# First stages of a three-block decoder kernel: the scan placed ahead of the last matrix powers, token weights computed in two halves, and the compression rows of batch 0 stored and loaded back ahead of the others

## Chip, cores and metric

The kernel runs on one core of a Trainium2 chip. The metric is device time in microseconds (us) of one execution, as the median of several. Times of single instructions come from a profile of one execution.

## What is computed

Three blocks follow each other, each ending in a layer normalisation over 256 features: an attention over 8192 key rows chosen by top-8, a cross attention with 16 heads, and a feed-forward block with token-to-expert selection. The change touches only the opening of the first block, which is (16 batches, 256 tokens, 256 features):

```python
xB = jnp.einsum('bsd,de->sbe', x, Bm)
def step(h, u):
    h = h @ A + u
    return (h, None)
h_final, _ = jax.lax.scan(step, h0, xB)
h_proj = h_final @ W_imp.T
importance = jax.nn.softmax(jnp.einsum('bsd,bd->bs', x, h_proj), axis=-1)
token_pref = jax.nn.softmax(jnp.einsum('bsd,nd->bsn', x, W_router), axis=-1)
neuron_w = jnp.einsum('bs,bsn->bn', importance, token_pref)
neuron_w = neuron_w / (neuron_w.sum(-1, keepdims=True) + 1e-08)
shared_compress = jnp.einsum('bn,ndr->bdr', neuron_w, compress)
Q = jnp.einsum('bsd,bdr->bsr', x, shared_compress)
scores = jnp.einsum('bsr,nr->bsn', Q, K) / math.sqrt(K.shape[1])
topk_scores, topk_idx = jax.lax.top_k(scores, kk)
```

## The kernel before

Every engine has its own instruction list, written out by hand, and waits on semaphores. The names: PE is TensorE, DVE VectorE, ACT ScalarE, POOL GpSimd, SP SyncE, which here only issues DMAs.

**The scan without a loop over 256 steps.** With RAD = 16, the scan is two sums of 16 terms. PE computes powers of A by doubling (`power(r)`, r = 0 to 7; r 0 to 3 give A to A^16, r 4 to 7 powers of A^16), and DVE copies each out of the accumulator before the next can start. `bm_powers` multiplies Bm by the first powers (`Bm_A_pow`), ACT copies. The first sum ("scan1", 32 matmuls over the input `xT_by_step`) gives `scan_partial`; the second ("scan2", 16 small ones with `A16_pow`) gives the final state. `warm(n)` issues n matmuls of 128x128 whose result nobody reads.

**Importance and router.** From the final state PE makes h_proj, then the importance logits ("imp", 32 matmuls). DVE takes their maximum, ACT the exponential, DVE the reciprocal and the product; PE transposes the result. Beside it runs the router: `router(n)` for four quarters n (two groups of batches by two token halves t), ACT copies it out (`router_out`), PE transposes it back, DVE takes the maximum and subtracts it, ACT takes the exponential (`router_exp`), DVE sums it (`router_sum`). Quarters 0 and 1 belong to token half t = 0, quarters 2 and 3 to t = 1. DVE multiplies importance by the reciprocal of the sum into `token_weight_diag`, for both halves, and PE sums over tokens ("nw", 32 matmuls, 16 for each half). A short chain on DVE and PE normalises that into `neuron_diag`.

**Compression.** 32 matmuls over eight loads of `compress` give, for each of 16 batches, two rows of 128x128 values: partition 32c + q of the result holds row q = 2 batch + k, for c = 0 to 3 (quarters of the row). ACT and DVE copy it in eight steps into `scs`, which lies in the space of `xT_by_step`. SP stores it to the DRAM tensor `shared_compress` (`scd`) with eight DMAs of 32 partitions (two halves by four c), and then loads the two rows of one batch back as `sc_in` in the shape in which PE needs it (`scd_v[0]` for batch 0, later one for each batch). Behind that load SP issues the loads of the projection weights.

**The main loop.** Turns c = -4 to 16 work on batches c, c+1, c+2 at once. The first thing that turn -2 does is `shared_q(0)`, which needs `sc_in` and `xT_in`; then come the 32 score blocks of batch 0 (three matmuls of 512 columns each), which ACT copies into `score_row` and of which DVE takes eight best per 2048 keys (`cand_val`, `cand_idx`). In the same turn ACT casts the six weight chunks (`weight_hi`), in order between its score copies: blocks 0 to 3, chunks 0 and 1, blocks 4 to 7, chunks 2 and 3. Three score banks lie between PE and ACT.

## Time and profile before

| | us |
|---|---|
| median of 3 runs | 1390.09 |
| lowest and highest | 1389.33 and 1392.59 |
| profiled execution | 1391.58 |
| span of its instructions | 1389.8 |
| PE busy | 1327.0 (95% of the span) |
| DVE busy | 1122.6 (81%) |
| ACT busy | 719.0 (52%) |
| POOL busy | 727.0 (52%) |

The page gives busy time per engine. "PEclk" or "granted clock" is the share of full speed that TensorE's clock gate passed; full is 2.4 GHz, half 1.2 GHz. The chain of waits follows the last instruction back to what released it, so it shows at each time which engine set the pace. An fp32 matmul stands in the trace as two passes, so 32 matmuls are "x64". The idle time behind "<-" is what the engine waited before an instruction and who ended that wait.

### The profile page before, as it was taken

What the parts mean: (1) busy time and instruction counts of PE and PEld (TensorE: products, weight loads), DVE (VectorE), ACT (ScalarE), POOL (GpSimd) and SP (SyncE); (2) the same over time, 40 slices, a digit from 0 to 9 for tenths busy, and PEclk for the clock granted to TensorE, in tenths of its full rate; (3) what the DMA queues carried; (4) which work ended last, traced back from release to release, by engine and by line L of the source; (5) the groups of instructions that cost most, each with busy time, mean ns of one, the idle gap of its engine ahead of it and who ended that gap; (6) DMA issues with size and microseconds to landing.
All of it is one profiled execution on the core that took longest, in us unless ns stands there. A gap on an engine that the chain in (4) does not pass through costs nothing.

```text
span 1389.8 us, 25203 instructions
## 1 busy us (share of the span) xinstructions
PE 1327.0 (95%) x9839; PEld 995.5 (72%) x9839; DVE 1122.6 (81%) x1627; ACT 719.0 (52%) x1377; POOL 727.0 (52%) x1009
## 2 busy tenths in 40 slices
PE   9856999999999999999999999999999999999898
PEld 4444868686868686868687868777878676867775
DVE  1459889898989898998898889898989986546567
ACT  1443565555555555555555555555555544336564
POOL 0543374747474746464646565656565646342434
PEclk9988999999999999999999999999999999999999
DMA  9462112222222222222223222212221216002412
GB/s 373 145 202 61 57 54 58 71 57 71 61 68 62 69 60 76 60 70 57 65 54 86 57 65 59 73 56 68 59 73 45 73 42 179 1 17 93 154 39 85
DMA packets 57548, 110.36 MB, mean 79 GB/s; under 512 B 9438, under 2 KB 38102, under 8 KB 56278
## 3 DMA queue, kind: packets, MB, share of 16 engines
q1 hardware_dynamic: 40342, 62.17, 14.7%
q0 software_dynamic: 14848, 41.96, 10.8%
q10 hardware_dynamic: 2240, 4.63, 0.9%
q8 instruction: 78, 1.28, 0.4%
q14 instruction: 40, 0.33, 0.1%
HBM read 98.50 MB, written 10.22 MB: 78 GB/s over the span
## 4 chain that ended last, share of the span: by engine, by line
PE 74%; DVE 13%; another core or an unknown queue 4%; POOL 3%; issue 3%; ACT 2%; DMA 1%; SPq 0%; POOLq 0%; ACTq 0%; DVEq 0%
PE side_bank L379 43%; PE score_bank L379 27%; DVE cand_val L1146 4%; DVE cand_idx L1149 4%; DVE x_sum L1172 2%; PE score_bank L748 2%; POOL exp L1397 1%; POOL v_rows L1369 1%; PE side_bank L748 1%; DVE den_recip L1197 1%; DVE top_weight L1168 1%; DVE dispatchedT L1307 1%; ACT exp L904 1%; DMA kT<-den_scratch 0%
## 5 line engine op out<-in xcount | busy, mean ns | idle before, releaser
L892 ACT COPY score_row<-score_bank 128x512 f32<-128x512 f32 x512 | 299.0, 591 | 112.9 <-PE score_bank L379 58.2
L1369 POOL DMA_INDIRECT v_rows<-in_V,top_idx x256 | 249.1, 973 | 130.3 <-issue 74.7
L1146 DVE MAX8 cand_val<-score_row 128x8 f32<-128x2048 f32 x128 | 291.7, 2279 | 30.1 <-ACT score_row L892 27.8
L1149 DVE FIND_INDEX8 cand_idx<-cand_val,score_row 128x8 uint32<-128x2048 f32 x128 | 292.5, 2285 | 0.0
L1397 POOL TENSOR_SCALAR exp<-exp,exp_bound 128x256 f32<-128x256 f32 x512 | 246.9, 498 | 85.6 <-ACT exp L904 84.0
L379 PE MATMUL score_bank<-keysT_hi,qT_hi 128*128 128x512 f32 x512 | 217.2, 424 | 20.6 <-ACT score_row L892 19.1
L379 PE MATMUL score_bank<-keysT_lo,qT_hi 128*128 128x512 f32 x512 | 205.2, 401 | 0.0
L379 PE MATMUL score_bank<-keysT_hi,qT_lo 128*128 128x512 f32 x512 | 204.7, 400 | 0.0
L904 ACT ACTIVATE exp<-side_bank 128x512 f32<-128x512 f32 x256 | 139.1, 595 | 94.4 <-PE side_bank L379 84.5
L379 PE MATMUL side_bank<-qT_heads,kT 64*128 64x256 f32 x1024 | 146.1, 404 | 3.4 <-ACT exp L904 3.4
L1172 DVE SCALAR_TENSOR_TENSOR x_sum<-v_rows,top_weight,x_sum 128x256 f32<-128x256 f32 x256 | 137.0, 535 | 9.4 <-DMA v_rows<-in_V,top_idx 0.3
L379 PEld LDWEIGHTS score_bank<-keysT_hi,qT_hi 128*128 128x128 f32 x512 | 97.8, 191 | 62.0 <-ACT score_row L892 24.3
L909 ACT COPY qT_heads<-side_bank 128x512 f32<-128x512 f32 x128 | 75.1, 587 | 111.5 <-PE side_bank L379 96.1
L379 PE MATMUL side_bank<-exp,v 128*64 128x256 f32 x1024 | 126.7, 388 | 1.1 <-POOL exp L1397 0.8
L379 PEld LDWEIGHTS side_bank<-qT_heads,kT 64*128 64x128 f32 x1024 | 88.6, 187 | 52.4 <-issue 40.9
L379 PE MATMUL side_bank<-wo,qT_heads 128*128 128x256 f32 x512 | 115.7, 379 | 0.8 <-ACT kT L909 0.8
L379 PEld LDWEIGHTS score_bank<-keysT_hi,qT_lo 128*128 128x128 f32 x512 | 98.0, 191 | 23.8
L1418 POOL TENSOR_TENSOR qT_heads<-qT_heads,kT 128x1024 f32<-128x1024 f32 x31 | 74.5, 2404 | 71.0 <-DMA kT<-den_scratch 70.2
L379 PEld LDWEIGHTS score_bank<-keysT_lo,qT_hi 128*128 128x128 f32 x512 | 98.2, 192 | 15.7
L379 PEld LDWEIGHTS side_bank<-wo,qT_heads 128*128 128x128 f32 x512 | 96.9, 190 | 15.3 <-issue 1.4
L1197 DVE RECIPROCAL den_recip<-score_bank 128x256 f32<-128x256 f32 x32 | 56.0, 1749 | 61.6 <-remote 52.8
L379 PEld LDWEIGHTS side_bank<-exp,v 128*64 128x64 f32 x1024 | 67.5, 137 | 52.4 <-issue 21.8
(200 smaller groups left out, 2282.1 us busy)
## 6 DMA issues: line engine op xcount, KB each, us to landing
kT<-den_scratch SPq DMA_DIRECT2D x62, 256.0 KB
...
keysT_raw<-in_KmT ACTq DMA_DIRECT2D x8, 512.0 KB, 10.6
...
```

The lines of the kernel that those rows point to most:

```text
L379: return nc.tensor.matmul(o, l, r, start=start, stop=stop, skip_group_check=True)
L748: last = nc.tensor.transpose(set2[n % 3][:, c0:c0 + P], dtt[:, n, k, :, g], idn[:, :])
L892: nc.scalar.copy(srow[n // PER % 2][:, i * CB:(i + 1) * CB], scb[n % 3]).then_inc(sem("score_evac"), 1)
L904: nc.scalar.activation(ex[i % NEX][:, :, :].rearrange("p k s -> p (k s)"), sp_[o][:, :], ACT.Exp, scale=A_SCALE).then_inc(sem("exp_done"), 1)
L909: nc.scalar.copy(to, job_bank(key)[:, :]).then_inc(free(key), 1)
L1146: own(nc.vector.max(cv[:, tile, cs], srow[g % 2][:, :]))
L1149: nc.vector.max_index(ci[:, tile, cs], cv[:, tile, cs], srow[g % 2][:, :]).then_inc(sem("cand_done"), 1)
L1172: own(nc.vector.scalar_tensor_tensor(acc[:, tile, :], vg[:, k, :], w8[:, tile, k:k + 1], acc[:, tile, :], ALU.mult, ALU.add))
L1197: nc.vector.reciprocal(rden[:, :], den).then_inc(sem("rden_done"), 1)
L1369: pool.indirect_dma_start(out=vg[:, k, :], out_offset=None, in_=V_rows, in_offset=bass.IndirectOffsetOnAxis(ap=i8[:, tile, k:k + 1], axis=0))\
L1397: last = nc.gpsimd.tensor_scalar(ex[i % NEX][:, k, :], ex[i % NEX][:, k, :], ub[:, k, c:c + 1], E_LO, ALU.min, ALU.max)
L1418: nc.gpsimd.tensor_tensor(qt[:, hs, :], qt[:, hs, :], kt[:, hs, :], ALU.mult)\
```

## The change

It changes the order of the lists and how the compression rows are stored; the arithmetic is the same.

- PE: both `bm_powers` come before `power(4)`, the scan is split in two (steps 0 to 7, 8 to 15) with `power(6)` between, and `power(7)` and `router(1)` come after it. `router(3)` moves behind h_proj, the transpose of quarter 2 into the middle of the importance matmuls. Of the early `warm` matmuls three are taken out; new ones stand before the importance transposes (3), before the transpose of neuron weights (3) and behind the compression (16).
- DVE: `scan_partial` is copied before the copy of `power(7)`. Reciprocal and token weights are computed by halves; the half t = 0 stands before `router(3)`.
- ACT: the key loads are issued before `router_out(1)`.
- SP: `xT_in` is loaded before `compress`. Each store is split into rows of batch 0 (2 partitions) and the other 30 partitions; `sc_in` waits for the 8 small stores, and the second half's large stores are issued behind it. The wait for all stores moves to SP before the turns and to ACT at turn -1, away from DVE. `kT` and `qT_heads` are allocated first among the main loop's tiles, which puts them over the space from which the stores read.
- The wait for all eight parts of `keysT_lo` becomes one wait per part at the first score blocks.

```diff
@@ -309,21 +309,29 @@
             for q in range(4):
                 h, bs = q // 2, slice(q % 2 * 8, q % 2 * 8 + 8)
                 sp.dma_start(xs[:, :, h, bs, :], xTs[:, :, h, bs, :]).then_inc(sem(f"xs_in{q}"), 16)
+            sp.dma_start(xt[:, :, :], xT[:, :, 0:S]).then_inc(sem("xt_in"), 16)
             for g in range(NG_SC):
                 sp.dma_start(comp_at[g], comp[:, g * CH:(g + 1) * CH]).then_inc(sem(f"comp_in{g}"), 16)
+            def store_rows(half, r0, r1, done):
+
+                for c in range(4):
+                    sp.dma_start(scd_st[half, c][r0:r1], scs[32 * c + r0:32 * c + r1, half * CH:(half + 1) * CH])\
+                        .then_inc(sem(done), 16)
+
             for half in range(2):
                 sp.wait_ge(sem("sc_act"), 2 * half + 2)
                 sp.wait_ge(sem("sc_dve"), 2 * half + 2)
-                for c in range(4):
-                    sp.dma_start(scd_st[half, c], scs[32 * c:32 * c + 32, half * CH:(half + 1) * CH])\
-                        .then_inc(sem("sc_stored"), 16)
-            sp.dma_start(xt[:, :, :], xT[:, :, 0:S]).then_inc(sem("xt_in"), 16)
-            sp.wait_ge(sem("sc_stored"), 16 * NG_SC)
+                store_rows(half, 0, KT, "sc0_stored")
+                if half == 0:
+                    store_rows(0, KT, B * KT, "sc_stored")
+            sp.wait_ge(sem("sc0_stored"), 16 * 8)
             sp.dma_start(sct[:, :, :], scd_v[0]).then_inc(sem("sct_in"), 16)
+            store_rows(1, KT, B * KT, "sc_stored")
             for n, (w, i, k) in enumerate(WCHUNKS):
                 sp.dma_start(wraw[:, 1, i, k, :], w[:, k * INNER:(k + 1) * INNER]).then_inc(sem(f"w_in{n}"), 16)
             sp.dma_start(wo[:, :, :], Wo).then_inc(sem("wo_in"), 16)
+            sp.wait_ge(sem("sc_stored"), 16 * 8)
             sp.wait_ge(sem("main_ready"), 1)
             for c in TURNS:
                 m, a, p = c + 1, c + 2, c - 1
@@ -424,47 +432,51 @@
                 last.then_inc(sem("routerT_pe"), 1)
             pe.wait_ge(sem("v_const"), 1)
-            warm(6)
+            warm(6, pp[0])
             pe.wait_ge(sem("A_in"), 32)
             for r in range(4):
                 power(r)
-                warm(1 + r // 2)
+                if r < 3:
+                    warm(1, pp[0])
+
+            def scan(steps):
+                for i in steps:
+                    for k in range(KT):
+                        last = mm(pp[0][k * SD:(k + 1) * SD, 0:B * RAD], ba[:, k, RAD - 1 - i, :],
+                                  xs_step[:, k, i // 8, i % 8, :, :], start=(i == 0), stop=(i == RAD - 1))
+                return last
+
             pe.wait_ge(sem("bmt_in"), 16)
             pe.wait_ge(sem("small_in"), 16 * 5)
+            pe.wait_ge(sem("pow_evac"), 4)
+            bm_powers(0)
+            bm_powers(1)
             power(4)
-            bm_powers(0)
-            power(5)
-            bm_powers(1)
-            power(6)
             pe.wait_ge(sem("ba_evac"), 2)
             pe.wait_ge(sem("xs_in0"), 16)
             router(0)
+            power(5)
+            pe.wait_ge(sem("ba_evac"), 4)
+            for q in range(1, 4):
+                pe.wait_ge(sem(f"xs_in{q}"), 16)
+            scan(range(0, 8))
+            power(6)
+            scan(range(8, RAD)).then_inc(sem("pre_pe"), 1)
             power(7)
-            pe.wait_ge(sem("xs_in1"), 16)
             router(1)
-            pe.wait_ge(sem("ba_evac"), 4)
-            pe.wait_ge(sem("xs_in2"), 16)
-            pe.wait_ge(sem("xs_in3"), 16)
-
-            for i in range(RAD):
-                for k in range(KT):
-                    last = mm(pp[0][k * SD:(k + 1) * SD, 0:B * RAD], ba[:, k, RAD - 1 - i, :],
-                              xs_step[:, k, i // 8, i % 8, :, :], start=(i == 0), stop=(i == RAD - 1))
-            last.then_inc(sem("pre_pe"), 1)
-            pe.wait_ge(sem("pow_evac"), 8)
-            router(2)
             router_transpose(0)
             pe.wait_ge(sem("pre_dve"), PRE_DVE["scan1_evac"])
+            pe.wait_ge(sem("pow_evac"), 8)
             for j in range(RAD):
                 last = mm(pp[1][0:SD, 0:B], qw[:, RAD - 1 - j, :], gt[:, :, j], start=(j == 0), stop=(j == RAD - 1))
             last.then_inc(sem("pre_pe"), 1)
-            router(3)
+            router(2)
             pe.wait_ge(sem("pre_dve"), PRE_DVE["scan2_evac"])
             for k in range(KT):
                 last = mm(pp[1][:, 32 + k * B:32 + (k + 1) * B], wit[:, k * P:(k + 1) * P], ht[:, :])
             last.then_inc(sem("pre_pe"), 1)
+            router(3)
             router_transpose(1)
-            router_transpose(2)
             pe.wait_ge(sem("pre_dve"), PRE_DVE["hm_evac"])
             for j in range(4):
                 for k in range(KT):
@@ -472,18 +484,22 @@
                         b = 4 * c + j
                         last = mm(pp[0][32 * c:32 * c + 32, 0:S], hm[:, k, b, :], xs[:, k, :, b, :],
                                   start=(j == 0 and k == 0), stop=(j == 3 and k == KT - 1))
+                if j == 1:
+                    router_transpose(2)
             last.then_inc(sem("pre_pe"), 1)
             router_transpose(3)
+            warm(3, pp[1])
             pe.wait_ge(sem("pre_dve"), PRE_DVE["imp_sm"])
             for t in range(TT):
                 last = nc.tensor.transpose(pp[1][:, t * P:(t + 1) * P], impe[:, t * P:(t + 1) * P], idn[:, :])
             last.then_inc(sem("pre_pe"), 1)
-            pe.wait_ge(sem("pre_dve"), PRE_DVE["uw_done"])
             for t in range(TT):
+                pe.wait_ge(sem("pre_dve"), PRE_DVE[f"uw{t}"])
                 for b in range(B):
                     last = mm(pp[0][0:B, 0:NC], uwd[:, t, b * B:(b + 1) * B], rte[:, t * B + b, :],
                               start=(t == 0 and b == 0), stop=(t == TT - 1 and b == B - 1))
             last.then_inc(sem("pre_pe"), 1)
+            warm(3, pp[1])
             pe.wait_ge(sem("pre_dve"), PRE_DVE["nw_done"])
             nc.tensor.transpose(pp[1][:, 0:B], nwd[:, :, :].rearrange("p o n -> p (o n)"), idn[0:B, 0:B])\
                 .then_inc(sem("pre_pe"), 1)
...
@@ -846,12 +864,12 @@
                     nc.scalar.copy(ba[:, k, 8 * hf:8 * hf + 8, :].rearrange("p a b -> p (a b)"), (sp_, pp)[hf][k][:, :])\
                         .then_inc(sem("ba_evac"), 1)
             router_out(0)
-            router_out(1)
             act.wait_ge(sem("xs_in3"), 16)
             for n in range(NK // KW):
                 act.dma_start(kraw[:, n * KW:(n + 1) * KW], KmT[:, n * KW:(n + 1) * KW]).then_inc(sem(f"k_in{n}"), 16)
             for dst, src in ((bob[:, :], bo), (cix[:, :, :], cidx), (mcu[:, :, :], mcol)):
                 act.dma_start(dst, src).then_inc(sem("main_const"), 16)
+            router_out(1)
             key_hi(0)
             router_out(2)
             router_exp(0)
...
@@ -1082,28 +1103,36 @@
                 last = nc.vector.tensor_copy(hm[:, k, :, :].rearrange("p (c j) m -> p c (j m)", j=4)[:, :, 0:4 * 32:33],
                                              pp[1][:, 32 + k * B:32 + (k + 1) * B].rearrange("p (c j) -> p c j", j=4))
             last.then_inc(sem("pre_dve"), 1)
+            def token_weights(t):
+
+                dve.wait_ge(sem("pre_pe"), PRE_PE["impT_pe"])
+                nc.vector.tensor_tensor(
+                    uwd[:, t, 0:B * B:B + 1].rearrange("p (c j) -> p c j", j=4),
+                    rrc[:, t * B:(t + 1) * B].rearrange("p (c j) -> p c j", j=4),
+                    pp[1][:, t * P:(t + 1) * P].rearrange("p (c m) -> p c m", c=4)[:, :, 0:4], ALU.mult)\
+                    .then_inc(sem("pre_dve"), 1)
+
+            def router_recip(t):
+                dve.wait_ge(sem("router_sum"), 2 * t + 2)
+                after("router_rec", nc.vector.reciprocal(rrc[:, t * B:(t + 1) * B], rsm[:, t * B:(t + 1) * B]), t + 1)
+
             router(1)
             router(2)
             router_sum(0)
-            router_sum(1)
             dve.wait_ge(sem("pre_pe"), PRE_PE["imp_pe"])
             nc.vector.tensor_reduce(imx[:, 0:1], pp[0][:, 0:S], AX, ALU.max, negate=True)\
                 .then_inc(sem("pre_dve"), 1)
-            router(3)
+            router_sum(1)
             dve.wait_ge(sem("imp_exp"), 1)
             after("imp_rec", nc.vector.reciprocal(imx[:, 2:3], imx[:, 1:2]), 1)
             nc.vector.tensor_scalar(impe[:, :], impe[:, :], imx[:, 2:3], None, ALU.mult).then_inc(sem("pre_dve"), 1)
+            router_recip(0)
+            token_weights(0)
+            router(3)
             router_sum(2)
             router_sum(3)
-            dve.wait_ge(sem("router_sum"), 4)
-            after("router_rec", nc.vector.reciprocal(rrc[:, :], rsm[:, :]), 1)
-            dve.wait_ge(sem("pre_pe"), PRE_PE["impT_pe"])
-            for t in range(TT):
-                last = nc.vector.tensor_tensor(
-                    uwd[:, t, 0:B * B:B + 1].rearrange("p (c j) -> p c j", j=4),
-                    rrc[:, t * B:(t + 1) * B].rearrange("p (c j) -> p c j", j=4),
-                    pp[1][:, t * P:(t + 1) * P].rearrange("p (c m) -> p c m", c=4)[:, :, 0:4], ALU.mult)
-            last.then_inc(sem("pre_dve"), 1)
+            router_recip(1)
+            token_weights(1)
             dve.wait_ge(sem("pre_pe"), PRE_PE["nw_pe"])
             after("nw_chain", nc.vector.tensor_reduce(nws[:, 0:1], pp[0][0:B, 0:NC], AX, ALU.add), 1)
             after("nw_chain", nc.vector.tensor_scalar(nws[:, 1:2], nws[:, 0:1], 1e-8, None, ALU.add), 2)
```

**PE around the scan.** Before, from the sixth power to the scan (`Wrouter_T` marks a router quarter, `Bm_A_pow` the scan):

```order
L379 MATMUL score_bank<-A_pow,AT_pow 128x256 [waits pow_evac]
L379 MATMUL score_bank<-AT_pow,A_pow 64x128
L379 MATMUL side_bank<-xT_by_step,Wrouter_T 64x512 [waits xs_in0,ba_evac]
L379 MATMUL side_bank<-xT_by_step,Wrouter_T 64x512 x3
L379 MATMUL score_bank<-A_pow,AT_pow 128x448 [waits pow_evac]
L379 MATMUL side_bank<-xT_by_step,Wrouter_T 64x512 [waits xs_in1]
L379 MATMUL side_bank<-xT_by_step,Wrouter_T 64x512 x3
L379 MATMUL side_bank<-xT_by_step,Bm_A_pow 64x256 [waits xs_in3,xs_in2,ba_evac]
L379 MATMUL side_bank<-xT_by_step,Bm_A_pow 64x256 x31
```

Now, from the first router quarter on:

```order
L387 MATMUL side_bank<-xT_by_step,Wrouter_T 64x512 [waits xs_in0,ba_evac]
L387 MATMUL side_bank<-xT_by_step,Wrouter_T 64x512 x3
L387 MATMUL score_bank<-A_pow,AT_pow 128x128 [waits pow_evac]
L387 MATMUL score_bank<-AT_pow,A_pow 64x128
L387 MATMUL side_bank<-xT_by_step,Bm_A_pow 64x256 [waits xs_in2,xs_in3,xs_in1,ba_evac]
L387 MATMUL side_bank<-xT_by_step,Bm_A_pow 64x256 x15
L387 MATMUL score_bank<-A_pow,AT_pow 128x256 [waits pow_evac]
L387 MATMUL score_bank<-AT_pow,A_pow 64x128
L387 MATMUL side_bank<-xT_by_step,Bm_A_pow 64x256 x16
L387 MATMUL score_bank<-A_pow,AT_pow 128x448 [waits pow_evac]
L387 MATMUL side_bank<-xT_by_step,Wrouter_T 64x512 x4
```

The scan stands one power and one router quarter earlier, and a power stands in its middle.

**DVE around the token weights.** Before, from the maximum of the importance logits:

```order
L1090 TENSOR_REDUCE imp_small<-side_bank 128x1 [waits pre_pe]
L1062 TENSOR_REDUCE router_max<-side_bank 128x8 [waits routerT_pe]
L1063 TENSOR_TENSOR router_exp<-side_bank,router_max 128x512 [waits router_max]
L1094 RECIPROCAL imp_small<-imp_small 128x1 [waits imp_exp]
L1095 TENSOR_SCALAR importance<-importance,imp_small 128x256 [waits imp_rec]
L1069 TENSOR_REDUCE router_sum<-router_exp 128x8 [waits router_exp] x2
L1099 RECIPROCAL router_recip<-router_sum 128x32 [waits router_sum]
L1102 TENSOR_TENSOR token_weight_diag<-router_recip,side_bank 128x16 [waits pre_pe,router_rec]
L1102 TENSOR_TENSOR token_weight_diag<-router_recip,side_bank 128x16
```

Now, from the same instruction:

```order
L1123 TENSOR_REDUCE imp_small<-side_bank 128x1 [waits pre_pe]
L1089 TENSOR_REDUCE router_sum<-router_exp 128x8 [waits router_exp]
L1127 RECIPROCAL imp_small<-imp_small 128x1 [waits imp_exp]
L1128 TENSOR_SCALAR importance<-importance,imp_small 128x256 [waits imp_rec]
L1117 RECIPROCAL router_recip<-router_sum 128x16 [waits router_sum]
L1109 TENSOR_TENSOR token_weight_diag<-router_recip,side_bank 128x16 [waits pre_pe,router_rec]
L1082 TENSOR_REDUCE router_max<-side_bank 128x8 [waits routerT_pe]
L1083 TENSOR_TENSOR router_exp<-side_bank,router_max 128x512 [waits router_max]
L1089 TENSOR_REDUCE router_sum<-router_exp 128x8 [waits router_exp] x2
L1117 RECIPROCAL router_recip<-router_sum 128x16 [waits router_sum]
L1109 TENSOR_TENSOR token_weight_diag<-router_recip,side_bank 128x16 [waits pre_pe,router_rec]
```

The first pair of `router_sum` is split around the maximum, and a reciprocal of 16 columns with one token weight stands ahead of the last router quarter.

**SP around the compression rows.** Before:

```order
L318 DMA shared_compress<-xT_by_step 32x4x512 [waits sc_dve,sc_act]
L318 DMA shared_compress<-xT_by_step 32x4x512 x3
L318 DMA shared_compress<-xT_by_step 32x4x512 [waits sc_dve,sc_act]
L318 DMA shared_compress<-xT_by_step 32x4x512 x3
L320 DMA xT_in<-in_xT 128x2x256
L322 DMA sc_in<-shared_compress 128x2x128 [waits sc_stored]
L324 DMA comp_then_wqkv_raw<-in_Wv 128x1024 x2
```

Now (the two-row and thirty-row forms are the split stores):

```order
L318 DMA shared_compress<-xT_by_step 2x4x512 [waits sc_dve,sc_act]
L318 DMA shared_compress<-xT_by_step 2x4x512 x3
L318 DMA shared_compress<-xT_by_step 30x4x512 x4
L318 DMA shared_compress<-xT_by_step 2x4x512 [waits sc_dve,sc_act]
L318 DMA shared_compress<-xT_by_step 2x4x512 x3
L328 DMA sc_in<-shared_compress 128x2x128 [waits sc0_stored]
L318 DMA shared_compress<-xT_by_step 30x4x512 x4
L331 DMA comp_then_wqkv_raw<-in_Wv 128x1024 x2
```

The number of store DMAs doubles to 16; 12 of them stand ahead of the load, of which 8 have two rows.

## Rows read from the trace of the kernel before

**Rows 1.** Chain of waits, 0 to 90 us: start, us, engine, tile, line
```profile
14.46 1.15 PE side_bank L379 x4
...
23.43 3.61 PE side_bank L379 x8
...
28.45 8.77 PE side_bank L379 x72
37.22 1.72 PE score_bank L379 x8
...
48.41 0.60 PE side_bank L423 x4
```

**Rows 2.** Timeline of DVE, 14 to 16 us: start, us, line, operation
```profile
15.30 0.21 DVE L1056 COPY A_pow<-score_bank 128x64 f32<-128x64 f32 x1
```

**Rows 3.** Busy time by stretch: us, engines (instructions), granted clock, DMA share, GB/s
```profile
48.40:51.84 3.44, 1.04 (x8) 0.56 (x6) 3.16 (x7) 1.92 (x4) 0.00 (x0) 1.00 0.00 0
51.84:58.66 6.82, 5.82 (x55) 5.82 (x56) 0.88 (x4) 4.94 (x6) 6.53 (x3) 0.50 0.00 0
58.66:68.30 9.64, 7.99 (x77) 2.62 (x74) 3.39 (x10) 2.35 (x4) 7.40 (x4) 1.00 0.18 39
72.31:78.50 6.19, 0.00 (x0) 0.00 (x0) 0.35 (x4) 0.00 (x0) 0.00 (x0) 0.50 0.76 207
78.50:85.97 7.47, 6.46 (x14) 4.63 (x15) 0.42 (x1) 1.72 (x4) 0.00 (x0) 0.50 0.96 342
```

**Rows 4.** Chain of waits, 49 to 69 us
```profile
49.04 0.70 DVE router_max L1062
...
50.56 0.35 DVE importance L1095
50.91 1.20 DVE router_sum L1069 x2
...
52.13 0.36 DVE router_recip L1099
...
52.84 6.52 PE side_bank L379 x64
...
61.19 7.12 PE score_bank L379 x64
```

**Rows 5.** The same stretches for instructions on the token weights alone (PE, PEld, DVE)
```profile
51.84:58.66 6.82, 5.82 (x55) 5.82 (x56) 0.27 (x2) 0.50 0.00 0
58.66:59.40 0.74, 0.68 (x12) 0.50 (x9) 0.00 (x0) 1.00 0.00 0
```

**Rows 6.** Groups by line, ACT, 40 to 60 us
```profile
L836 ACT ACTIVATE router_exp<-router_exp 128x512 f32<-128x512 f32 x4 | 2.5, 630 | 4.1 <-DVE router_exp L1063 4.1
```

**Rows 7.** Timeline of SP, 65 to 83 us, the stores' issue
```profile
65.68 7.22 SPq L318 DMA_DIRECT2D shared_compress<-xT_by_step  x8
```

**Rows 8.** Chain of waits, 69 to 79 us
```profile
71.89 4.26 DMA shared_compress<-xT_by_step
...
76.17 2.23 DMA sc_in<-shared_compress
```

**Rows 9.** Timeline of SP, 194 to 197 us: a store of 8 KB, then the load that awaits it
```profile
194.65 0.63 SPq L358 DMA_DIRECT2D den_scratch<-den_recip  x1
196.42 1.15 SPq L362 DMA_DIRECT2D kT<-den_scratch  x2
```

**Rows 10.** DMA of 195.6 to 196.2 us, in which only that store moved
```profile
DMA packets 10, 0.01 MB, mean 14 GB/s; under 512 B 2, under 2 KB 10, under 8 KB 10
```

**Rows 11.** DMA issues of 0 to 100 us: KB each, median us to landing
```profile
comp_then_wqkv_raw<-in_Wv SPq DMA_DIRECT2D x2, 512.0 KB, 4.9
```

**Rows 12.** Timeline of ACT, 86 to 92 us: the first two weight chunks
```profile
87.13 2.00 ACT L877 CAST wqkv_hi<-comp_then_wqkv_raw 128x1024 fp32r<-128x1024 f32 x2
```

**Rows 13.** Busy time by stretch, columns as in rows 3
```profile
90.00:139.50 49.50, 33.27 (x112) 23.87 (x110) 48.45 (x57) 23.70 (x45) 26.10 (x20) 0.86 0.20 61
140.60:144.01 3.41, 3.41 (x9) 2.67 (x8) 3.38 (x4) 1.15 (x2) 2.50 (x4) 0.50 0.31 89
```

20 lines of the change are left out of this document (12 added, 8 removed).

## Prediction

> **What bounds the kernel now.** I read the page first (the busy table: PE 95% of the span), then the chain of waits for the opening, then busy time by stretch for the clock, then the timelines of the queues. The change acts before 80 us, where the page's average says little, so the chain decides. It shows four stages in which one thing alone sets the pace. (1) Up to 49.0 us PE is on the chain without a break [rows 1]: warm matmuls, powers, router quarters, the scan, the importance matmuls. Nothing but less PE work, or faster PE work, shortens it. (2) From 49.0 to 61.2 DVE and PE alternate in the token weights and their normalisation [rows 4]. (3) From 61.19 the compression takes PE 7.12 us [rows 4]; then the stores and the reload of batch 0 take until 78.4: the last store is issued at 71.89 and lands 4.26 us later, `sc_in` needs 2.23 us more [rows 8]. PE does nothing in 72.31 to 78.50 [rows 3]. (4) After the first scores DVE is busy 48.45 of the 49.5 us from 90 to 139.5 [rows 13]; then PE sets the pace to the end. Stages 1 to 3 feed one chain, stage 4 starts when they are done and consists of fixed DVE work. So a microsecond taken from stages 1 to 3 should arrive at the end, unless something else that stage 4 needs comes late.
>
> **The clock** matters as much as the order. A router quarter of eight passes takes 3.61 us at 23.43 but 1.72 us at 37.22 [rows 1]: the first ran at 1.2 GHz, the second at 2.4 GHz. The granted clock fell at 51.84 after a stretch in which PE was busy 1.04 of 3.44 us, was at half until 58.66, fell again by 72.31 and was half until 85.97 [rows 3].
>
> **Part 1, PE up to the importance logits: 1.9 us gained.** Removing warm matmuls: the four passes at 14.46 took 1.15 us, but the next power may not start before DVE has copied the last one at 15.30 + 0.21 = 15.5 [rows 2], which is where it started before. The same happens one power earlier, where one of two is removed. The copies move forward with the shorter second pause, so I take 0.45 us, not the 1.7 us of removed work. The rest of the list up to the logits is the same work in another order, and PE has something to do while DVE copies a power, as it had before; so reordering alone is worth nothing here. But the first router quarter now follows directly behind the Bm powers: powers 5 and 6 (together some 2.5 us at half clock) no longer precede it, so it starts near 20.6 instead of 23.43, and behind one short power comes the scan. Before, the full rate came about 4.5 us after the first router quarter began, at 27.9: the powers ahead of it, 64-row matmuls with PE on the chain all the time, had not raised the clock in 20 us. The same 4.5 us now give 25.0, so 2.9 us of half clock become full clock and save half, 1.45 us. Bounds: nothing, if the clock rises when it did; 2.4 us, if it rises with the quarter's end. Logits end at 48.4 - 1.9 = 46.5.
>
> **Part 2, token weights by halves: 3.2 us.** Count from the end of the logits, T (before 48.41 [rows 1]). Before, nw starts at 52.84, T + 4.4, since DVE did the last router quarter (0.70 + 0.69) [rows 4], the product (0.35), two sums (1.20), reciprocal (0.36) and two multiplications before it, and it runs at half clock: 6.52 us, end T + 10.95. Now maximum, exponential, reciprocal and product end at T + 2.0 (the last router quarter is out of it, a sum of 0.6 hides behind ACT); transposes, a half reciprocal and one multiplication give nw's first half at T + 2.7. For the second half DVE still owes router quarter 1.4, ACT's exponential 0.63 [rows 6], a sum 0.6, half reciprocal 0.3, multiplication 0.2, so it may start at T + 5.9. A half of 32 passes at full clock takes 32 x 0.056 = 1.8 us (twelve passes in 0.68 us [rows 5]), at half 3.3. At full clock nw ends at T + 7.7, at half T + 9.3. Which? Before, the fall came with 1.04 us of work in 3.44; the pause between nw and the compression (59.4 to 61.2, one short transpose) left it full [rows 3]. Now the gaps behind T are about 0.7, 0.3 and 1.3 us, with transposes, three warm matmuls and the first half between them. That is nearer to the second row, so I take full: 10.95 - 7.7 = 3.2 us; low end 1.6.
>
> **Part 3, the stores: 0.9 us.** Count from the compression's start, C (before 61.19). The first half is copied out at C + 4.5 and its first store is issued then (65.68 [rows 7]); the second half at C + 7.9. Before, the last store lands at C + 15.0. Now twelve issues stand ahead of the load. Small ones: the nearest row is the 8 KB store to `den_scratch`, 0.63 us of issue and 1.77 us until the load that waits for it is issued [rows 9]. Large ones stand at 7.22 / 8 = 0.9 us [rows 7], of which part is the queue being full. Issues: 4 x 0.6 + 4 x 0.8 + 4 x 0.6 = 8.0, last issued at C + 12.5, landing C + 13.7 if nothing is queued. Data: eight stores of 256 KB took from the first issue, 65.68 [rows 7], to 71.89 + 4.26 = 76.15 [rows 8]; less about 0.9 us for the start that is 1.2 us each. The large stores of half 0 start behind the small ones, at C + 7.7, and need 4 x 1.2 = 4.8, to C + 12.5; then the four small ones of half 1. The den store left ten packets, eight of data and two short ones [rows 10], which I read as two DMA engines working on a store with two outer rows. Four such stores put 16 packets of 2 KB on each of two engines: at 1.2 us / 8 = 0.15 us a packet 2.4 us, alone perhaps 0.09. So they land between C + 13.9 and C + 15.2; I take C + 14.1, gain 0.9. Bounds: -0.3 and +2.0. The reload stays 2.23.
>
> The Trainium skill, "DMA: Bandwidth & Descriptors", section "Why a DMA increments its semaphore by 16 and not by 1", says that the number of DMA engines is the largest one up to 16 which divides the slowest dimension of both sides, so 2 for a store of two rows and 15 for thirty; that speaks against this form of the change. The trace agrees for the den store (its two short packets). If instead the rows were spread over all 16 engines, the small stores would cost 0.3 us and Part 3 would be worth about 1.9.
>
> `xT_in` was issued while SP waited for the stores, so it was never what PE waited for; placed ahead of `compress` it delays those loads by under 1 us, and no DMA runs in 48.40 to 58.66 [rows 3], so they end over 10 us before their use at 61.19. The weight loads now stand behind four large stores: Wv lands 4.9 us after issue [rows 11], before near 76.6 + 4.9 = 81.5 = C + 20.3, now near C + 23. ACT casts it at 87.13, C + 25.9 [rows 12], 25.0 after Part 3's gain, so it is covered by some 2 us. The one wait less on DVE and the key parts' own waits have long been met: nothing.
>
> **Part 4, warm matmuls behind the compression: 0.** 32 passes of 128 columns at full clock last some 3.5 us, to C + 10.6; the product for batch 0 comes at C + 16.4. That leaves 5.8 us of idle PE. Before, the clock was half 4.0 us after the last matmul. So it falls again and the first scores run at half as before (6.46 busy in 78.50 to 85.97 [rows 3]). Bounds: +3.2 if it stays full, -1 if its rise falls later.
>
> **Sum.** 1.9 + 3.2 + 0.9 = 6.0 us. Against the profiled execution, 1391.58 - 6.0 = 1385.6; it stood 1.5 above the median of the three runs, so against 1390.09 it is **1384.1 us**.
>
> **Rivals.**
> - *The early clock does not come earlier*: if what raised it at 27.9 was not the router quarter's 128-row matmuls but plain elapsed time, Part 1 is 0.45. Sum 4.6, 1385.5. For it: only one rise is in view. Against: 20 us of powers did not raise it.
> - *The clock falls inside nw*: between the halves PE waits 1.3 us and nw's 64-column passes are small. Then Part 2 is 1.6, sum 4.4, 1385.7; with the first rival too, 3.0, 1387.1.
> - *The clock is held up through the reload, or the stores land early*: +2 to +3, 1381.5. For it: the warm matmuls halve the pause. Against: 5.8 us is over the 4.0 after which it fell.
> - *Slower: weights come late.* ACT casts chunks 0 and 1 between score blocks 3 and 4. If Wv lands late, ACT stands at its cast, three score banks fill, PE stops, and DVE, which sets the pace [rows 13], runs out of rows. Each us later than C + 26 in landing costs one us beyond DVE's slack of 0.7 us. The kernel is slower from a landing at about C + 33, 10 us behind my estimate; at C + 36 it is 1393. The four large stores and two small loads ahead of Wv would have to move at a third of the rate seen.
> - *Given back later*: what runs at half clock in stage 4 depends on where its pauses fall. PE work of 3.41 us at 140.60 ran at half and was on the chain [rows 13]; it may vanish or come twice, +-1.7.
>
> **How the numbers follow.** Forecast 45%; early clock unchanged 17%; clock falls in nw 13%; both 5%; held clock or early stores 17%; slower 3%. A measurement of this kernel can tell about 0.3%, 4.2 us, from no change: the border of faster is 1385.9. The forecast with +-1.7 has some 85% below it, the two single rivals about 60%, both together 20%, the held clock all. That gives 0.75 faster, 0.22 same, 0.03 slower. The range takes in the held clock and both clock rivals: 1380.8 to 1387.4.
>
> **What would show it.** In the changed profile: `router_T` matmuls at 1.72 us for eight passes before 27 us, and logits ending near 46.5; DVE `router_recip` twice, the first before the last `router_max`, nw's 64 passes in two groups of 1.8 us with granted clock 1.00; comp matmuls starting near 56; `sc_in` issued 14 us after them; a granted clock of 0.50 at the first scores; the first weight cast near 81.1 instead of 87.13. A cast at 81 with the end not earlier would mean that stage 4 gave it back.

## The result

The changed kernel takes 1379.69 us (median of 4 runs, 1377.70 to 1380.99), the kernel before 1389.71 in the same comparison (4 runs, 1386.37 to 1392.59). The ratio is 0.9928 with a 95% interval of 0.9916 to 0.9941, so the gain is 10.0 us where 6.0 were forecast; the time lies 1.1 us under the range. Two more comparisons of the same two kernels gave ratios of 0.9935 [0.9915, 0.9956] and 0.9938 [0.9915, 0.9960]. The chips differ: the kernel before took 1379.75, 1387.96 and 1387.91 us on the three that the experiments ran on, so times are compared only within one of them.

The page's summary of the chain of waits has PE at 88% of it (74% before) and the unattributed part at 2% (4%):

```profile
PE 88%; DVE 5%; issue 2%; another core or an unknown queue 2%; ACT 2%; DMA 0%; SPq 0%; POOL 0%; POOLq 0%; ACTq 0%; DVEq 0%
```

The profiled execution of the changed kernel took 1377.70 us (span 1375.8), that of the kernel before 1391.58 (1389.8). These two differ by 13.9 us, more than the medians do; 9.4 us of it are there by the first candidates (the first `cand_val`), and the rest is dealt with below. All profile lines have the columns of the sections ahead of the prediction; the helper that records every matmul is line 387 here, 379 before.

The chain of waits of the changed kernel, up to the logits (compare [rows 1]):

```profile
15.00 0.14 DVE A_pow L1076
15.14 0.14 issue
15.27 3.39 PE side_bank L387 x8
18.66 0.51 PE score_bank L387 x4
19.17 1.87 PE side_bank L387 x8
21.04 0.77 PE score_bank L387 x4
21.81 3.60 PE side_bank L387 x32
25.42 0.98 PE score_bank L387 x4
26.40 3.60 PE side_bank L387 x32
30.00 0.95 PE score_bank L387 x2
```

The eight passes at 15.27 are the Bm powers. The first router quarter (eight passes at 19.17) takes 1.87 us instead of 3.61, and each power behind it less than a microsecond: the clock is already at its upper level. The clock's record has its first rise at 18.13 (27.94 before, after 12.29 us from 15.65 in which PE was busy without a break). One caution: ahead of the first change that a record holds, the granted-clock column reads 1.00 even where passes take twice their time, so up to there the durations are what to read. From 18.13 PE is busy without a break at full clock, and the logits' last matmul ends at 44.45, where before it ended at 48.41 [rows 1].

The token weights and the stores, from the same view:

```profile
50.19 1.98 PE side_bank L387 x32
...
53.99 3.69 PE score_bank L387 x32
...
58.48 0.31 SPq L318
...
58.84 0.23 SPq L318
...
61.63 1.14 SPq L318
...
64.05 3.14 DMA shared_compress<-xT_by_step
67.20 2.16 DMA sc_in<-shared_compress
...
69.50 2.06 PE side_bank L387 x4
...
72.53 4.72 PE score_bank L387 x12
...
77.89 2.31 DVE cand_val L1174
```

The second half of nw is 32 passes in 1.98 us (before, 64 in 6.52 [rows 4]). The four small stores from 58.48 are issued in 0.23 to 0.42 us each. The first candidates are taken at 77.89; before, at 87.27.

The clock by stretch, PE being the first figure (compare [rows 3]):

```profile
46.98:53.99 7.01, 5.02 (x71) 4.45 (x71) 4.26 (x13) 5.71 (x7) 4.07 (x2) 1.00 0.03 10
53.99:62.00 8.01, 8.01 (x73) 2.98 (x74) 2.94 (x5) 2.94 (x5) 8.01 (x5) 1.00 0.17 41
64.84:69.33 4.49, 0.00 (x0) 0.00 (x0) 0.00 (x0) 0.00 (x0) 0.00 (x0) 1.00 0.33 94
69.33:76.16 6.83, 5.68 (x13) 4.04 (x14) 0.42 (x1) 1.54 (x3) 0.00 (x0) 0.50 0.88 222
```

Through nw it stays full. Behind the 16 warm matmuls PE is idle from 64.84, and the clock falls at 69.33, just before the first scores. The weights, on ACT:

```profile
77.76 1.05 ACT L895 CAST wqkv_hi<-comp_then_wqkv_raw 128x1024 fp32r<-128x1024 f32 x1
79.02 1.04 ACT L895 CAST wqkv_hi<-comp_then_wqkv_raw 128x1024 fp32r<-128x1024 f32 x1 [0.21 <-DMA comp_then_wqkv_raw<-in_Wv]
```

The second cast waits 0.21 us for its weights (they land at 77.74 and 79.00), so the cover that I put at 2 us is used up.

### The profile page after: what moved, and what is told of

Read it like the earlier page. It is cut to its first block, busy times and chain, and to the rows that moved or that the text cites. A ratio compares the mean times of both kernels' runs of the same rounds, so it can differ in the third digit from the quotient of the medians.

```text
span 1375.8 us, 25304 instructions
## 1 busy us (share of the span) xinstructions
PE 1321.6 (96%) x9877; PEld 993.5 (72%) x9877; DVE 1125.4 (82%) x1628; ACT 718.8 (52%) x1377; POOL 728.9 (53%) x1009
## 4 chain that ended last, share of the span: by engine, by line
PE 88%; DVE 5%; issue 2%; another core or an unknown queue 2%; ACT 2%; DMA 0%; SPq 0%; POOL 0%; POOLq 0%; ACTq 0%; DVEq 0%
PE side_bank L387 51%; PE score_bank L387 33%; PE score_bank L766 2%; DVE cand_idx L1177 1%; DVE cand_val L1174 1%; PE side_bank L766 1%; DVE dispatchedT L1335 1%; PE side_bank L548 1%; ACT exp L922 0%; PE score_bank L606 0%; ACT score_row L910 0%; SPq L318 0%; DVE x_sum L1200 0%; POOL exp L1425 0%
## 5 line engine op out<-in xcount | busy, mean ns | idle before, releaser
L1397 POOL DMA_INDIRECT v_rows<-in_V,top_idx x256 | 249.0, 973 | 130.8 <-issue 74.5
L1200 DVE SCALAR_TENSOR_TENSOR x_sum<-v_rows,top_weight,x_sum 128x256 f32<-128x256 f32 x256 | 134.2, 524 | 9.1
```

The costliest lines, as they stand in the source:

```text
L1200: own(nc.vector.scalar_tensor_tensor(acc[:, tile, :], vg[:, k, :], w8[:, tile, k:k + 1], acc[:, tile, :], ALU.mult, ALU.add))
L1397: pool.indirect_dma_start(out=vg[:, k, :], out_offset=None, in_=V_rows, in_offset=bass.IndirectOffsetOnAxis(ap=i8[:, tile, k:k + 1], axis=0))\
```

## The experiments

Four kernels ran on each of three chips, beside the kernel before. "Rise" is the time at which the clock becomes full after the long stretch at half with which the opening begins, T the end of the logits, C the start of the compression. Medians are over 4 to 10 executions of a kernel; the four columns of times come from one profiled execution each.

| kernel | chip | median us (before there) | ratio [95%] | rise | T | C | first candidates |
|---|---|---|---|---|---|---|---|
| before, first profile | | | | 27.94 | 48.41 | 61.19 | 87.27 |
| changed, first profile | | 1379.69 (1389.71) | 0.9928 [0.9916, 0.9941] | 18.13 | 44.45 | 53.99 | 77.89 |
| b_bm | 1 | 1379.27 (1379.75) | 0.9997 [0.9988, 1.0007] | 27.58 | 48.90 | 61.27 | 87.08 |
| a_split | 1 | 1372.63 | 0.9956 [0.9939, 0.9972] | 22.7 | 45.87 | 55.41 | 78.80 |
| b_halves | 1 | 1375.85 | 0.9979 [0.9970, 0.9989] | 25.87 | 46.50 | 56.02 | 81.79 |
| b_stores | 1 | 1377.57 | 0.9985 [0.9975, 0.9995] | 28.33 | 48.61 | 61.48 | 84.81 |
| a_again | 2 | 1379.05 (1387.96) | 0.9935 [0.9915, 0.9956] | 18.99 | 43.89 | 53.44 | 77.94 |
| a_nowarm | 2 | 1381.29 | 0.9950 [0.9932, 0.9967] | 18.44 | 44.61 | 54.15 | 77.90 |
| a_warm36 | 2 | 1379.77 | 0.9937 [0.9918, 0.9956] | 19.16 | 43.98 | 53.52 | 74.80 |
| a_rest_last | 2 | 1377.80 | 0.9927 [0.9906, 0.9947] | 19.85 | 45.24 | 54.79 | 76.43 |
| b_front | 3 | 1387.04 (1387.91) | 0.9987 [0.9974, 1.0000] | 20.02 | 47.89 | 60.40 | 86.18 |
| b_part1 | 3 | 1383.37 | 0.9964 [0.9950, 0.9979] | 19.84 | 45.24 | 57.27 | 82.91 |
| a_third | 3 | 1380.28 | 0.9938 [0.9915, 0.9960] | 20.42 | 45.48 | 55.03 | 79.48 |
| a_combo | 3 | 1375.92 | 0.9910 [0.9887, 0.9934] | 21.39 | 45.96 | 55.51 | 74.70 |

In some profiles (a_split, a_again, a_warm36, b_halves) the clock was also full for a few microseconds before 9 us, and a_again and a_warm36 have T 0.9 us earlier than the other profiles of their order would have at that rise; such profiles are left out where T is set against the rise below.

**What raises the clock: b_bm, a_split, b_front.** The kernel before with the two groups of Bm powers next to each other:

```
-            power(4)
+            pe.wait_ge(sem("pow_evac"), 4)
             bm_powers(0)
-            power(5)
             bm_powers(1)
+            power(4)
+            power(5)
             power(6)
```

> The kernel before with one edit: the two groups of Bm powers stand together ahead of power 4, so PE has eight passes of 512 columns in a row. Theory 1 (that row of wide passes is what raised the clock at 18.1 us in the changed kernel): the granted rate doubles near 19 us here too, the first router quarter takes about 1.8 instead of 3.6 us, the importance logits end near 44.5 instead of 48.4, and the run is 3 to 4 us faster. Theory 2 (my prediction: the router quarter's 128-row matmuls raise it): the quarter still starts near 23.4 and takes 3.6 us, the rate doubles near 28, logits end at 48.4, no change of time.

The rise came at 27.58, where it was, and the time did not move (ratio 0.9997), so theory 1 falls for a row of Bm passes alone. The Bm powers are in one piece, at 15.65 to 19.44, but behind them PE waits for DVE's copies between the powers:

```profile
15.65 3.78 PE side_bank L379 x8
19.44 0.91 PE score_bank L379 x4
...
20.38 0.23 DVE A_pow L1052
20.60 0.20 DVE AT_pow L1055
...
20.85 1.42 PE score_bank L379 x4
...
22.29 0.29 DVE A_pow L1052
22.58 0.20 DVE AT_pow L1055
...
22.83 1.83 PE score_bank L379 x4
24.66 3.33 PE side_bank L379 x8
```

The changed kernel with power 4 between the two Bm groups:

```
             bm_powers(0)
-            bm_powers(1)
             power(4)
+            bm_powers(1)
```

> The changed kernel with one edit: power 4 stands between the two groups of Bm powers again, so that no eight wide passes stand in a row. Theory 1 (the row of wide passes raises the clock): the clock no longer rises near 18 us but only behind the router quarter, near 24; logits end 2 to 3 us later (46.5 to 47.5 instead of 44.4), the run 2 to 3 us slower than the changed kernel. Theory 2 (router quarter or plain elapsed time): the clock as in the changed kernel, logits near 44.5, no change.

The router quarter began at 18.51 and ran at the lower rate; the rise came at 22.7. The clock by stretch:

```profile
18.50:22.10 3.60, 3.60 (x10) 0.77 (x8) 0.00 (x0) 1.07 (x2) 0.00 (x0) 0.50 0.99 412
22.70:27.00 4.30, 4.30 (x37) 2.64 (x36) 0.48 (x2) 0.12 (x1) 0.00 (x0) 1.00 1.02 422
```

That is 4.2 us behind the quarter's start, close to the prediction's 4.5. The other profiles with the Bm groups apart have 4.2 to 4.9 as well (b_halves, before, b_stores); b_bm has 2.9. Where both Bm groups and the router quarter follow each other with one power between, that count does not hold: the rise comes before or during the quarter. Counted from the first Bm pass it is 2.9 to 6.1 us there, in nine profiles, and 9.1 in a_split. T came 2.0 us later than in a_again, which also has the early full spell; 46.5 to 47.5 was expected, 45.87 came. The changed kernel did not run on this chip, and by the ratios (0.9956 against 0.9928 to 0.9938) the intervals overlap, so the 2 to 3 us of time are neither shown nor refuted. The kernel before with only the Bm groups and the first router quarter ahead of power 5:

```
-            power(4)
+            pe.wait_ge(sem("pow_evac"), 4)
             bm_powers(0)
-            power(5)
             bm_powers(1)
-            power(6)
+            power(4)
             pe.wait_ge(sem("ba_evac"), 2)
             pe.wait_ge(sem("xs_in0"), 16)
             router(0)
+            power(5)
+            power(6)
             power(7)
```

> The kernel before with one edit in TensorE's order: both groups of Bm powers and the first router quarter stand ahead of A^32, so that power 4 alone is between them; everything behind (scan, router quarters, token weights, stores) is as before. Theory (it is the uninterrupted run of 512-column Bm and router matmuls that raises the granted clock, not the number of matmuls): the clock is first full for good between 18.5 and 20.5 us, where grouping the Bm powers alone left it at 27.58; the first router quarter starts near 19.5 and takes about 1.9 us instead of 3.6, the scan still waits for power 6, and the logits end near 44.5 to 45.5 instead of 48.4 to 48.9. Rival 1 (the prediction's: only the 128-row router matmuls raise the clock, some 4.5 us behind their start): full at 24, logits at 46.5 to 47. Rival 2 (the early rise of the changed kernel comes from its shorter opening, one warm matmul fewer behind the powers): clock near 27, logits near 48. The time of the whole kernel: 1 to 3 us below the kernel before in the theory's case, of which the intervals can show the upper part only.

The rise was at 20.02, as the theory said, and the router quarter took 1.87 us. Order alone raises the clock 8 us earlier, with as many matmuls as before. But my number for the logits was wrong: 47.89, only 0.5 us earlier than before, and the kernel's time moved by 0.9 us, which its interval can't tell from nothing. Two views of b_front show why, the chain and the clock by stretch:

```profile
20.25 1.87 PE side_bank L379 x8
22.11 0.79 PE score_bank L379 x4
22.90 0.03 issue
22.93 0.29 DVE A_pow L1052
...
23.46 1.07 PE score_bank L379 x4
...
24.55 0.42 DVE A_pow L1052
...
26.24 10.47 PE side_bank L379 x72
```

```profile
20.02:26.90 6.88, 5.60 (x24) 2.08 (x24) 2.13 (x7) 1.12 (x3) 0.00 (x0) 1.00 1.02 424
26.90:30.30 3.40, 3.40 (x14) 1.24 (x12) 0.00 (x1) 0.59 (x1) 0.00 (x0) 0.51 1.02 419
30.30:36.70 6.40, 6.40 (x62) 4.29 (x60) 0.00 (x0) 0.00 (x0) 0.00 (x0) 1.00 1.00 411
```

At full clock the powers are too short to cover DVE's copies: PE waits 0.56 us (22.90 to 23.46) and then again from 24.53. And after a stretch with 5.60 us of work in 6.88 the clock fell at 26.90 for 3.40 us, inside the scan (its 72 passes took 10.47 us, 8.77 before [rows 1]). In this profile the early clock by itself is worth little: the waits and the fall together take most of it back.

**Part 1 alone: b_part1.** The kernel before with the whole new order up to the logits (Bm groups, router quarter, scan in two pieces with powers 5, 6 and 7 between and behind, the router quarters after it, and what ACT and VectorE do in that order) and without the three early warm matmuls, nothing else:

```
+            power(5)
+            pe.wait_ge(sem("ba_evac"), 4)
...
+            scan(range(0, 8))
+            power(6)
+            scan(range(8, RAD)).then_inc(sem("pre_pe"), 1)
             power(7)
             router(1)
```

> The kernel before with the whole first part of the change alone (Bm groups and router quarter ahead of the powers, the scan ahead of the last two powers, router quarters moved behind it, ScalarE's and VectorE's order of it), without the warm matmuls, halves or stores of the others. Theory (the early clock is most of this part, the removal of powers from the way to the scan the rest): logits end between 43.9 and 45.5, the clock full from 18 to 20 us; kernel 3.5 to 5 us below the kernel before, if what is gained ahead is kept. Rival (a prediction of 1.9 us for this part): logits near 46.5, kernel 1.5 to 2.5 us below. Rival 2 (the part's gain is lost when the token weights' passes, without the halves, meet a half clock): logits early, compression rows still near 60.

T is 45.24 and the kernel 4.5 us faster, as the theory said; the first candidates come 4.4 us earlier than in the first profile of before (87.27; b_bm has 87.08, so this does not hang on the chip). The rival of 1.9 us falls. Against b_front, T is 2.65 us earlier at the same rise (19.84 and 20.02). 0.37 of that is the shorter front (the Bm passes start at 15.28 instead of 15.65); the rest comes with the order behind the quarter, which puts halves of the scan in front of the last powers, so that PE neither waits nor drops its clock before T.

**The halves and the stores alone: b_halves, b_stores.** In b_halves only the token weights go by halves (`uw0`, `uw1` and DVE's order):

```
             for t in range(TT):
+                pe.wait_ge(sem("pre_dve"), PRE_DVE[f"uw{t}"])
                 for b in range(B):
```

> The kernel before with the token weights by halves alone (DVE's order and PE's two waits; the added warm matmuls and the new place of the transposes are left out). If the halves carry part 2 by themselves: the sum over tokens ends about 1.6 us after where it would at half clock, that is at logits + 9.3 instead of + 10.9, gain 1.6 us. If the clock stays full because of the denser work: + 7.7, gain 3.2 us. If the added warm matmuls are needed for the clock, the first holds.

nw began at T + 2.52 and ended at T + 7.68, at full clock without the extra warm matmuls. From T to C it took 9.52 us (12.78 before), 3.26 less. The time fell by 3.9 us by the medians, 2.9 by the ratio; 3.2 lies between them. T itself lies 1.9 us earlier than before in this profile; the halves come behind it and can't have done that, the earlier clock can (a full spell before 9 us and a rise at 25.87).

In b_stores the order of the stores is the changed one, with `xT_in` ahead, the moved waits and the new places of `kT` and `qT_heads`:

```
-                for c in range(4):
-                    sp.dma_start(scd_st[half, c], scs[32 * c:32 * c + 32, half * CH:(half + 1) * CH])\
-                        .then_inc(sem("sc_stored"), 16)
+                store_rows(half, 0, KT, "sc0_stored")
+                if half == 0:
+                    store_rows(0, KT, B * KT, "sc_stored")
```

> The kernel before with the new order of stores and reload alone (split stores, xT_in ahead of the compression loads, the moved waits). The changed kernel's trace has the last small store land 13.2 us after the compression starts instead of 15.0. If that is the store order's own doing, the gain here is 1.8 us and the reload is issued at 61.2 + 13.2 = 74.4 instead of 76.17; my prediction had 0.9. If it came with the other parts, the landing is at 75.3 or later.

`sc_in` was issued at 74.19, C + 12.71 (C + 15.0 before), as expected from the store order's own doing, and the time fell by 2.2 us (ratio 0.9985, 2.1 us). SP's own row shows where my 8.0 us of issue went: twelve issues in 6.16 us.

```profile
65.97 6.16 SPq L318 DMA_DIRECT2D shared_compress<-xT_by_step  x12
74.19 0.40 SPq L328 DMA_DIRECT2D sc_in<-shared_compress  x1
```

**The whole again: a_again, a_third.** The changed kernel unedited, on the second and the third chip.

> The changed kernel itself, unedited, beside the kernel before on the same chip as the three runs with it. The sum of the stages read so far (logits 2 to 4 us earlier, token weights 3.2, stores 2.0, first scores 0.3) gives 7.5 to 9.5 us. My prediction's sum was 6.0. If the first comparison's 10.0 us held something of the main loop's own, the gain here is nearer to 8.

> The changed kernel unedited, so that parts and whole stand on one chip. If the parts add up: gain of the whole = this call's gain of part 1 + 3.2 (halves, where they run at full clock) + 1.8 (stores) = 8 to 10 us; if they cover each other (the first cast of the weights waits), less than 8. Opening as in the profiles before: clock full from 18 to 20, first small store near 58, first scores at half clock, first candidates 77.5 to 78.5.

By the ratios the parts are worth 5.0 (b_part1), 2.9 (b_halves) and 2.1 us (b_stores), together 10.0; the whole was worth 10.0, 9.0 and 8.6 us in three comparisons. The intervals reach 1.3 to 3.1 us to either side, so they add up as far as these runs can tell. That a_third's first candidates would come at 77.5 to 78.5 was a miss: 79.48, since its clock rose 2.3 us later than in the first profile (T 1.0 later) and its fall, at 68.2, lasted 10.2 us where it had been 6.8.

**The warm matmuls behind the compression: a_nowarm, a_warm36.** Without the 16, and with 36 in their place:

```
-            warm(16, pp[1])
+            warm(36, pp[1])
```

> The changed kernel without the 16 warm matmuls behind the compression. Prediction's part 4 (they are worth nothing): the granted clock is half at the first scores with and without them, the time between the product for batch 0 and the first candidate search stays 8.4 to 8.7 us, no change of the run. Rival (they keep the clock up into the product or bring its rise forward): 0.3 to 1 us slower without them.

> The changed kernel with 36 warm matmuls behind the compression instead of 16, enough at 0.12 us a pass (32 took 3.84 us) to reach the arrival of batch 0's rows. If the clock is what holds the first scores back, it stays full, the product and the first four score blocks take half as long, and the first candidate search comes 8.4 - 3 = 5.4 us behind the product: 3 us faster, unless the weights' first chunk, which already is 0.2 us late in the changed kernel, takes part of it: then 1 us faster. If the warm matmuls overrun the arrival, the product starts later by the overrun.

Without them the opening is no longer: 8.64 us from the product for batch 0 to the first candidates against 9.04 in a_again, the clock half from 66.2 to 76.5 (66.8 to 77.0). The kernel was 2.2 us slower by the medians, more than the rival's 0.3 to 1, but the intervals of the ratios overlap. The difference in the profiles lies between the start of batch 0's V (the first matmul on `wqkv_hi` and `ctx_hi`) and the last exponential (1091.7 against 1088.7 us). There the clock is half for 6.8 us from 1131 on, against 3.4 in a_again, which is worth 1.7 us at most; what brings it about, and the rest, stays open. With 36 the clock stayed full up to 80.6 and the first candidates came 3.1 us earlier, at 74.80, and yet the time did not move (1379.77 against 1379.05). Where the gain went, ACT's row says:

```profile
76.78 1.04 ACT L895 CAST wqkv_hi<-comp_then_wqkv_raw 128x1024 fp32r<-128x1024 f32 x1 [2.01 <-DMA comp_then_wqkv_raw<-in_Wv]
78.03 1.05 ACT L895 CAST wqkv_hi<-comp_then_wqkv_raw 128x1024 fp32r<-128x1024 f32 x1 [0.21 <-DMA comp_then_wqkv_raw<-in_Wv]
```

ACT stood at the first cast for 2.01 us until the weights had landed. The second row of candidates was only 1.4 us earlier (81.24 against 82.63), batch 0's V 0.65 us (130.41 against 131.06). A wait that the slower scores had hidden took the place of the one removed.

**The large stores last: a_rest_last.** All eight large stores go behind the reload and the six weight loads:

```
                 store_rows(half, 0, KT, "sc0_stored")
-                if half == 0:
-                    store_rows(0, KT, B * KT, "sc_stored")
             sp.wait_ge(sem("sc0_stored"), 16 * 8)
...
+            for half in range(2):
+                store_rows(half, KT, B * KT, "sc_stored")
```

> The changed kernel with all large stores issued behind the reload and behind the six weight loads. Theory: the small stores of the second half wait in their queues behind 1 MB of large stores; without those they land some 3 us after the second half is copied out (C + 7.9), near C + 11 instead of C + 13.2, the pause of PE is under 3 us and the clock stays full: the first candidate search comes 2 us earlier by the stores and up to 3 us by the clock, 2 to 5 us faster. Rival: the small stores are bound by their own 16 packets on two engines and by their issue; then they land near C + 12.5 and the gain is under 1 us.

`sc_in` was issued at C + 11.08 instead of C + 13.25, and Wv had landed at 70.3 and 72.2, over 4 us before its first cast. So the small stores did wait for the large ones, and the rival (C + 12.5) falls. The theory's other half failed: PE paused for 2.6 us, under 3 as expected (warm matmuls to 65.64, the product at 68.25), and yet the clock fell at 67.64 and was half until 74.47. V of batch 0 began at 129.93 (131.06), though T was 1.35 us later in this profile. The median is 1.25 us lower than a_again's, under the 2 to 5 expected, and within the intervals.

**Both together: a_combo.** a_rest_last with 28 warm matmuls:

```
-            warm(16, pp[1])
+            warm(28, pp[1])
```

> The changed kernel with two edits together: all large stores behind the reload and the six weight loads (alone: 1377.8 against 1379.05, weights landed at 70.3 and 72.2), and 28 instead of 16 warm matmuls behind the compression (36 alone: clock held to 80.6, first candidates 3.1 us earlier, but the gain went into the wait for the weights). Theory (the two are each other's missing half): the clock stays full through the first scores, the first candidates come at 73.5 to 74.5, the first weight cast finds its weights landed, V of batch 0 starts about 2.5 to 3 us earlier than with the large stores last alone, and the kernel is 3 to 4.5 us below the changed one. Rival (the main loop's own pace, not the opening, sets what is kept; or a dip of the clock comes later instead): first candidates at 74 as well, but the kernel no more than 1.5 us below the changed one.

Each takes away what had eaten the other's gain. The warm matmuls now reach up to the product for batch 0, the clock stayed full, and the twelve first score matmuls took 3.08 us, not 5.29 as in a_third (4.72 in the first profile of the changed kernel):

```profile
63.00:68.89 5.89, 5.89 (x54) 5.87 (x54) 2.63 (x5) 0.00 (x0) 2.43 (x2) 1.00 0.22 55
70.97:74.05 3.08, 3.08 (x13) 2.53 (x14) 0.00 (x0) 1.76 (x3) 0.00 (x0) 1.00 0.96 326
```

```profile
74.56 2.00 ACT L894 CAST wqkv_hi<-comp_then_wqkv_raw 128x1024 fp32r<-128x1024 f32 x2
76.46 2.24 ACT L909 COPY score_row<-score_bank 128x512 f32<-128x512 f32 x4
```

Both casts of the second view run back to back with no wait. The first candidates came at 74.70 (a_third 79.48), just behind the stretch I expected; V of batch 0 began at 128.29 (132.59), and the median was 4.4 us below a_third's, 12.0 below before's: the fastest version that was run on its chip. The forecast of 3 to 4.5 us under the changed kernel held. Counted from C, which leaves out the spread of T, V of batch 0 starts at 77.6 us in a_again and in a_third, 76.9 with 36 warm matmuls, 75.1 with the large stores last and 72.8 with both: 4.8 us together where the two alone have 0.7 and 2.5.

## Why the prediction was off, step by step

The direction, the four stages and two of the four terms were right. The time came out 4.4 us under the forecast. 3.4 us of that are terms that were too small, parts 1 and 3 above all; 0.4 is the median of the kernel before, which was lower in the comparison (1389.71 against 1390.09); 0.6 no term accounts for. By events of the first two profiles, of the 9.4 us at the first candidates:

| part | forecast | measured |
|---|---|---|
| 1: up to the logits (T) | 1.9 | 3.96 (48.41 to 44.45) |
| 2: T to the compression's start | 3.2 | 3.24 (12.78 to 9.54) |
| 3: compression's start to the product for batch 0 | 0.9 | 1.83 (17.34 to 15.51) |
| 4: from there to the first candidates | 0 | 0.35 (8.74 to 8.39) |

**Part 1: the step that failed is "the same 4.5 us now give 25.0".** I ascribed the one rise in view to the router quarter's 128-row passes and gave the 512-column passes of the Bm powers ahead of it no share, because 20 us of powers had not raised the clock. But those 20 us held no long run of such passes without a power between them. In the changed order the rise was at 18.13, in all eight profiles of that order between 18.1 and 21.4. b_front shows that order alone does it, 20.02. Counted from the first Bm pass at 15.27 instead of from the quarter, my own 4.5 us would have given 19.8. What it is in this order that raises the clock, the runs narrow down (the quarter has to follow the joined groups, b_bm; the groups have to be joined, a_split) but don't settle further. My bound for this, 2.4 us if the clock rose with the quarter's end, was too tight, since it could rise before the quarter began.

A second error went the other way. Six profiles of the new order without an early full spell give T against the rise: 44.45 (18.13), 44.61 (18.44), 45.24 (19.84 and 19.85), 45.48 (20.42), 45.96 (21.39), which is 0.46 us of T for each microsecond of the rise. Extended to 25.0 this line gives T = 47.6, not my 46.5: an extrapolation, but it says that with my clock the part would have given less than I claimed, and that 6.9 us of earlier clock brought 3.2. The front itself gained 0.38 (PE at 15.27 instead of 15.65), for which I had 0.45. "Reordering alone is worth nothing here" was wrong for the clock that came: b_front against b_part1, at an equal rise, differ by 2.65 us in T, 0.37 of it the front. At full clock, as b_front shows, the old order behind the quarter leaves PE with too little to do while DVE copies a power.

**Part 2** came as written: nw ends at T + 7.7 at full clock, in the changed kernel and in b_halves. The rival, that the clock falls inside nw, happened in no profile of the halves; in b_part1, which has none, it fell at 50.6 and from T to C took 12.03 us (a_third 9.55).

**Part 3: the mis-sized term is the issue of the small stores.** I took 0.6 us each from the 8 KB store to `den_scratch` [rows 9]; in the row of twelve they took 0.23 to 0.70, the eight together 3.0 us instead of 4.8, and all twelve 6.26 us instead of 8.0. The first four took 1.4 us, not 2.4, so the large stores behind them started earlier and the last of them landed at C + 11.9 instead of C + 12.5. The last small store, issued by C + 10.8 and not C + 12.5, still had to wait for them: it landed 1.3 us behind them, where I had 1.6, and the reload went out at C + 13.2 (forecast C + 14.1). The order of events was as forecast, the size was not. With no large store ahead, a_rest_last has the reload at C + 11.1: the four large stores of half 0 in front of the last small ones still cost 2 us. The value lies inside my bounds, near the upper one. The alternative with the small stores spread over all engines did not come: in the changed profile the eight 2 KB packets of a small store move at most two at a time.

**Part 4**: the clock fell before the first scores, as forecast. The reason that I gave was not a good one: I took a pause longer than 4.0 us as what makes it fall, but in a_rest_last it fell 2.0 us after the last matmul, in a_again after 2.5, in the first profile of the changed kernel after 4.5 and in a_nowarm after 5.0. The weights were covered by nothing instead of 2 us. Counted from C, the first cast came at C + 23.8 where I had C + 25.0, because the product and the first scores came earlier, and Wv landed at C + 23.8 and C + 25.0 where I had C + 23 for both. A time that I took as safe became the limit because other terms were better than I thought and this one a little worse. a_warm36 shows that it was one.

**What the stages keep.** That a microsecond from the opening arrives at the end held where nothing else was late: 4.4 us at the first candidates and 4.5 in the time (b_part1), 2.5 and 2.2 (b_stores), 9.4 and 10.0 (the whole), 4.8 and 4.4 (a_combo against a_third). It did not in a_warm36, 3.1 and nothing, where the weights were late. The profiled executions differ by more because stage 4 itself varies: from V of batch 0 to the last exponential 1092.0 us in the first profile of before and 1087.2 in that of the changed kernel, 1095.2, 1089.3, 1088.7 and 1086.9 in those of the third chip, in the order of the table. Of that, the clock explains little. Both kernels have a half-clock stretch of 3.4 us at the start of V (140.6 before, 130.8 in the changed kernel), the one that the last rival thought might vanish; only a later one, 3.4 us at 1144.1, is missing in the changed profile, and it is worth 1.7 us at most. The rest of the 4.8 us stays open. The first of the three chips speaks against the change as its cause: there the same stretch took 1080.6 to 1080.9 us in all four kernels, with the changed order (a_split) and without, and none of them has a fall of the clock between 144 us and the last 10 us. V of batch 0 started 8.3 us earlier in a_split than in b_bm, and their profiled executions differ by 7.7. The same rows show that this chip is faster than the others in the main loop and not in the opening (V of batch 0 at 140.2 in b_bm, 140.4 in the first profile of before).
